# Linear attention: transposes in place of four-column fp32 matmuls for key sums and normaliser, and stages that end without GpSimd's drain

## What is computed

```python
q = hidden_states @ Wq.T + bq
k = hidden_states @ Wk.T + bk
v = hidden_states @ Wv.T + bv
...
sq = elu_plus_one(q)
sk = elu_plus_one(k)
kv = jnp.einsum('bhsd,bhse->bhde', sk, v)
qkv = jnp.einsum('bhsd,bhde->bhse', sq, kv)
k_sum = sk.sum(axis=2)
norm = jnp.einsum('bhsd,bhd->bhs', sq, k_sum)
attn = qkv / (norm[..., None] + EPS)
...
return attn @ Wo.T
```

## Time and profile before

| what | us |
|---|---|
| median of three runs | 1677.63 |
| lowest and highest run | 1674.96, 1680.66 |
| profiled execution: span from first to last instruction | 1676.2 |
| TensorE busy in it | 1602.2 |
| VectorE busy | 1156.1 |
| GpSimd busy | 637.4 |
| ScalarE busy | 414.9 |

### The profile page before, as it was taken

How to read it: one execution, slowest core, us unless ns; L and a number is a source line. 1 busy time by engine, 2 the same in 40 slices (tenths; PEclk the granted TensorE clock), 3 DMA queues, 4 the chain that set the end, 5 groups by cost and what they waited for, 6 DMA issues and landing times. The chain is left out here.

```text
span 1676.2 us, 20502 instructions
## 1 busy us (share of the span) xinstructions
PE 1602.2 (96%) x6768; PEld 1134.1 (68%) x6768; DVE 1156.1 (69%) x1641; ACT 414.9 (25%) x706; POOL 637.4 (38%) x473
## 2 busy tenths in 40 slices
PE   6999988999999989979999999999999999999997
PEld 3444456566576566558877878777776677888886
DVE  5889788788888898565537777787877556252423
ACT  2333231111111111123233333333332222121211
POOL 3686646465665576530023323232332332010101
PEclk9999999999999999999999999999999899999999
DMA  5434878755756754332200000000005433011010
GB/s 198 169 111 175 296 251 248 236 202 212 242 194 201 242 194 171 138 113 76 94 20 20 20 20 26 13 26 19 13 11 183 116 119 143 9 48 52 19 57 25
DMA packets 84388, 197.87 MB, mean 118 GB/s; under 512 B 6864, under 2 KB 28112, under 8 KB 75984
## 3 DMA queue, kind: packets, MB, share of 16 engines
q1 hardware_dynamic: 84160, 196.28, 35.0%
q10 hardware_dynamic: 144, 0.52, 0.1%
HBM read 154.83 MB, written 41.94 MB: 117 GB/s over the span
## 5 line engine op out<-in xcount | busy, mean ns | idle before, releaser
L2003 DVE SCALAR_TENSOR_TENSOR l_acc<-l_ps,l_inv,l_acc 128x512 f32<-128x512 f32 x240 | 166.1, 747 | 6.1 <-PE l_ps L768 6.1
L2530 DVE CAST g_x_part<-g_x 128x512 fp32r<-128x512 f32 x64 | 37.1, 580 | 185.0 <-ACT g_x L2582 185.0
L1879 POOL TENSOR_TENSOR relay<-l_expq,l_reluq 128x512 f32<-128x512 f32 x42 | 55.4, 1318 | 188.6 <-ACT l_expq L2163 188.6
L766 PE MATMUL r_ps<-relay_part,entry 128*128 128x512 f32 x256 | 104.8, 410 | 15.0 <-DVE r_h L1193 5.2
L2458 POOL TENSOR_TENSOR relay<-relay 128x512 f32<-128x512 f32 x16 | 21.7, 1354 | 256.0 <-DVE relay L2510 256.0
L1074 POOL TENSOR_TENSOR r_rS<-r_S,first_r 128x512 f32<-128x512 f32 x64 | 94.5, 1479 | 57.9 <-DVE r_S L1178 57.9
L1074 POOL TENSOR_TENSOR r_rS<-r_S,r_rT 128x512 f32<-128x512 f32 x64 | 95.2, 1487 | 55.8 <-DVE r_S L1178 55.1
L1979 DVE TENSOR_SCALAR l_expq<-l_ps,l_bq 128x512 f32<-128x512 f32 x64 | 48.0, 751 | 86.6 <-ACT l_reluq L2159 86.6
L766 PE MATMUL g_ps<-g_Wdn,g_x_part 128*128 128x512 f32 x256 | 103.7, 405 | 0.0
L766 PE MATMUL l_ps<-l_M_part,l_sq_part 128*128 128x512 f32 x256 | 101.8, 398 | 0.8 <-DVE l_acc L2003 0.8
L768 PE MATMUL r_ps<-relay_part,entry 128*128 128x512 f32 x256 | 101.3, 396 | 0.0
(11 more groups left out here) (332 smaller groups left out, 4081.0 us busy)
## 6 DMA issues: line engine op xcount, KB each, us to landing
entry<-scratch_wgu SPq DMA_DIRECT2D x32, 1024.0 KB, 6.1
V<-scratch_v SPq DMA_DIRECT2D x96, 256.0 KB
relay<-scratch_x SPq DMA_DIRECT2D x15, 1024.0 KB, 7.8
r_w_part<-scratch_wgu SPq DMA_DIRECT2D x12, 1024.0 KB, 7.1
scratch_wgu<-f_halves SPq DMA_DIRECT2D x24, 384.0 KB, 5.0
relay<-scratch_v SPq DMA_DIRECT2D x32, 256.0 KB
relay<-in_x SPq DMA_DIRECT2D x4, 1024.0 KB, 7.8
scratch_x<-f_xT SPq DMA_DIRECT2D x4, 1024.0 KB, 6.7
```

The costliest lines, as they stand in the source:

```text
L766: nc.tensor.matmul(out, left[1], right[0], start=start, stop=False)
L1879: nc.gpsimd.tensor_tensor(sq[i % N_SQ], expq[i % 2][:, :], reluq[i % 2][:, :], ALU.add).then_inc(sq_ready, 1)
L2003: last = nc.vector.scalar_tensor_tensor(acc[b][:, t, :], ps, scale, acc[b][:, t, :], ALU.mult, ALU.add)
L2530: nc.vector.tensor_copy(hi[:, :], x2[j % 2][:, :]).then_inc(x2_hi_ready.sem, 1)
```

## The change

The key sums and the turned rows come from four transposes each, 128 by 128, that fill a whole bank. What the stationary or moving column picked before is picked by the reader now: line 1986's operation reads every 32nd of the 512 columns (`P // B` is 32), 16 values as before. For the key sums, VectorE reads every 32nd column as four heads by four tiles and adds the four (`key_sums`, a new function), which replaces both ScalarE's copy and the constant `every` with its reduction and its semaphore. Its places in VectorE's stream are: before `values(b)` for the batch before, and for the last batch after the second `minimum` of the second part. Allocations behind `every` move by 32 bytes per partition.

```diff
-        block = ctx.enter_context(nc.Block())
+        block = ctx.enter_context(nc.Block(no_gpsimd_drain=True))
...
+            def key_sums(b):
+                dve.wait_ge(*product("ksum", b))
+                by_part = place("ksum", b)[:, 0:KVH * D:P // TT].rearrange("p (g t) -> p g t", t=TT)
+                nc.vector.tensor_reduce(ksum[b][:, :], by_part, AX.X, ALU.add).then_inc(ksum_ready, 1)
...
-                nc.vector.tensor_scalar(flat(norm[h % 2][:, :, :]), place("turn", h)[:, 0:TT * B], 1e-6, None,
+                nc.vector.tensor_scalar(flat(norm[h % 2][:, :, :]), place("turn", h)[:, 0:TT * P:P // B], 1e-6, None,
                                         ALU.add).then_inc(norm_ready, 1)
...
-            nc.vector.tensor_reduce(every[:, :], ident[:, 0:P:32], AX.X, ALU.add).then_inc(every_ready, 1)
...
+                if b > 0:
+                    key_sums(b - 1)
                 values(b)
...
+                if i == 1 - LEAD:
+                    key_sums(B - 1)
...
-            def copy_ksum(b):
-                act.wait_ge(*product("ksum", b))
-                nc.scalar.activation(ksum[b][:, :], place("ksum", b)[:, 0:KVH], ACT.Copy).then_inc(ksum_ready, 1)
...
-                if b > 0:
-                    copy_ksum(b - 1)
...
-                if i == 1 - LEAD:
-                    copy_ksum(B - 1)
...
-                    pe.wait_ge(every_ready, 1)
                     pe.wait_ge(krow_ready, n + 1)
                     for g in range(KVH):
-                        last = nc.tensor.matmul(out[:, g:g + 1], gathered[:, g * D:(g + 1) * D], every[:, :],
-                                                start=True, stop=True)
+                        last = nc.tensor.transpose(out[:, g * D:(g + 1) * D], gathered[:, g * D:(g + 1) * D], ident[:, :])
...
                     for t in range(TT):
-                        last = nc.tensor.matmul(out[:, t * B:(t + 1) * B], gathered[:, t * P:(t + 1) * P],
-                                                ident[:, 0:P:32], start=True, stop=True)
+                        last = nc.tensor.transpose(out[:, t * P:(t + 1) * P], gathered[:, t * P:(t + 1) * P], ident[:, :])
```

More of the change, by code:

```diff
@@ L1671, in linear_attention @@
         ones = sb("ones", [P, 32])
-        every = sb("every", [P, 1])
         half = sb("half", [P, TT])
@@ L1720, in linear_attention @@
         kvT_lo_ready = sem("kvT_lo_ready")
-        every_ready = sem("every_ready")
         krow_ready = sem("krow_ready")
```

## The result

The changed kernel takes **1668.76 us** (median of ten runs, 1664.67 to 1675.62), against 1677.78 us for the kernel before (ten runs beside them, 1674.37 to 1680.99). By the medians that is 9.0 us less, where 9.2 were forecast. The ratio, worked out over the runs and not from the two medians, is 0.9954 with a 95% interval of 0.9941 to 0.9966: 7.7 us less, somewhere between 5.7 and 9.9. So it is faster by 0.34 to 0.59%; that the medians meet the forecast to a few tenths of a microsecond is closer than these runs can resolve.

The account below looks back on a forecast made before the run. The prediction took TensorE in the attention to bound the kernel: -9.4 us for 20 groups, 0 for VectorE, +0.2 for barriers, -9.2 in all. That gave 1668.4 us, range 1663.5 to 1673.0.

Parts of the forecast that it names:

- What bounds the kernel: In the attention, TensorE sets the pace: a microsecond less for it is one off the end if nobody becomes late.
- The group of transposes, 0.82 to 0.35: At each turn and key sum, TensorE's group falls from 0.82 to 0.35 us, 0.47 us less.
- 20 groups, -9.4: 16 turns and 4 key sums at 0.47 us each: 9.4 us less on TensorE, bounds 7.6 to 9.6.
- VectorE, zero: In the attention, VectorE's new reductions and strided norm operation cost nothing; reductions without cover 0.8 us, at worst 1.6.
- Barriers, +0.2: At the ends of stages, the changed barriers add 0.2 us in all, bounds 0 to +0.5.
- The sum and the time: Whole kernel: -9.4 + 0 + 0.2 = -9.2 us, forecast 1668.4 us, 0.55% less.
- The clock rival: After groups of transposes the granted clock falls to 1.2 GHz; about 1718 us if after each of 20; 3%.
- VectorE does not take over: Rival judged: VectorE takes TensorE's place at each turn, giving back up to 0.47 us at 20 places; 6%.
- the transposes are one record each: Rival judged: transposes run as fp32 matmuls in two records, +1 us in all, 1678.8 us; 2%.
- the drain was not on the path: Rival judged: GpSimd's drain held back the barriers, at most 3.4 us at each of four ends; 2%.
- the low-clock stretches give something back: Rival: the half-clock stretch at the last stage's start shifts, with over 4.5 us given back; 9%.
- Marks that failed as they were worded: Signs: equal barrier distances, last stage starting about 9.2 us earlier, no stage outside the attention changing over 1 us.

Follow-up runs that it names:

- transposes_only: The changed kernel with the old ends of stages (GpSimd's drain kept): 1665.73 us, ratio 0.9941 to the kernel before.
- the empty blocks: The changed kernel with 20 empty blocks behind the last stage: 1674.82 us with GpSimd's drain, 1676.64 us without it.
- transposes_twice: The changed kernel with each of the 20 groups of four transposes issued twice into the same bank: 1676.12 us, ratio 1.0001 to the kernel before.
- barrier_only: The kernel before with only GpSimd's drain removed at all four blocks: 1677.2 us, ratio 1.0002 to the kernel before.
- matmuls_twice: The kernel before with each of the 20 groups of four narrow fp32 matmuls issued twice: 1696.35 us, ratio 1.0116 to the kernel before.

## Why the prediction was right, point by point

- **What bounds the kernel.** Right. 0.47 us less for TensorE at a head is 0.47 us less for the head (26.775 to 26.305, group start to group start). Nobody became late. The doubled groups show it from the other side.
- **The group of transposes, 0.82 to 0.35.** Right to 0.01 us: 0.35 and 0.36 in the trace. The row with the same neighbours on both sides was the one to take. The lower bound of 0.38 gained, from a long run of transposes, is what a second group costs, not the first.
- **20 groups, -9.4.** 9.4 on the ruler with the barriers kept (transposes_only). The 26.83 us of the forecast between turns was a small misreading. The first and last start of the earlier trace rows are those of the group's first and of its last record; from group start to group start it is 26.775 us. The difference hid in both kernels' rows alike.
- **VectorE, zero.** Right, though one reason was not read from the rows: that the last batch leaves VectorE more room. TensorE waits 0.9 us for VectorE's values just there, behind the third reduction. The wait is the same after the change and even with 4.1 us more ahead of it, so the reduction is free there too. The reduction takes 0.17 us, and two whole-bank reductions more before it cost nothing either. The norm operation with its stride did not become slower: 165 ns where it had 174. The idle 0.42 us ahead of the first accumulation went, and nothing else did.
- **Barriers, +0.2.** The sign and the reason were right, the term was too small: +0.3 by the two barriers round the attention (4 x 0.08), +0.4 by the empty blocks, within its bounds. 0.05 us had been put on an event with its dispatch, which no row gave; it is 0.08 to 0.1. The removal of the drain gains nothing, since SyncE is last.
- **The sum and the time.** -9.4 and +0.3 to +0.4 are -9.0 to -9.1; the medians say -9.0, the ratio -7.7 with an interval of -5.7 to -9.9. The forecast of 1668.4 is 0.4 from the median of 1668.76. That closeness is in part luck, since the ten runs of before spread over 6.6 us and those of after over 11; what carries the terms is the ruler.
- **The clock rival.** Refuted. The heads are at 1.00, with four and with eight transposes in a row. The rule of the Trainium skill (TensorE: Matmul & The Clock Gate, Part 4: PE-mode transpose), that transposes do not count as activity like matmuls, is not borne out by these runs; had it held in the way of that rival, transposes_twice would have shown it first. No run here has more than sixteen transposes in a row, so what a long stretch of them alone would do is not shown.
- **The other rivals.** VectorE does not take over; the transposes are one record each; the drain was not on the path (barrier_only 1.0002). That the low-clock stretches give something back: in the profiled execution, yes, but in the wrong place. The last stage is 2.1 us shorter there, not longer, and the front and the recurrence are 6.9 us longer.
- **Marks that failed as they were worded.** The distances at the barriers are not equal: 0.08 us longer. Two more failed by much. "The start of the last stage about 9.2 us earlier" is 1.9 us (1287.9 to 1286.0), and the front and the recurrence did not stay as long as they were. Both compare two single executions across stages that the change leaves alone, and the low-clock time differed there by some 20 us. By the forecast's own words a change of over 1 us outside the attention would have counted against it. The marks should have been set within the attention.

By mechanism the best version is transposes_only: the same groups, with barriers that are 0.1 us shorter. Its 1665.73 us (five runs) and after's 1668.76 can't be told apart by their intervals, and 0.3 to 0.4 us is all that the rows account for.

## What to carry to other kernels

To pick a few columns out of a tile on an engine that is full, a transpose of the whole tile can be cheaper than a narrow fp32 matmul, if the reader can pick the columns instead: compare the two by the time to the next product's start, in a place with the same neighbours. An engine that waits a long time in its drain costs nothing while another arrives later; look at who arrives last before taking the drain out. When a gain is under a per cent, measure between marks inside the changed stage, from the same record of each group.

## What the runs showed of the hardware

- A barrier without GpSimd's drain is dearer than one with it when GpSimd is idle: 0.44 us against 0.33. Behind stages it is 0.08 us dearer too, with SyncE last to arrive. An idle GpSimd's DRAIN takes 34 ns, where one after the recurrence took 3006 ns.
- Four fp32 matmuls with four columns run as eight records and cost 0.82 us between wide products, 0.89 us when they follow another such group. Four fp32 transposes with 128 columns cost 0.35 us, 0.44 us when they follow others.
- Reading 16 values per partition from PSUM with a stride of 32 took VectorE 165 ns, 16 neighbouring ones 174 ns.
- The granted clock can fall in a full stream of matmuls: in the profiled execution of matmuls_twice it was 0.50 for 3.4 us behind the last sixteen records of narrow matmuls, and products with 512 columns stood 0.43 us apart in place of 0.23. It was seen once, and its cause is open.
- The scatter between executions goes with stretches at half clock: in the ten runs of the changed kernel, from a span of 1662.9 us at a mean clock of 0.991 to 1673.8 us at 0.985. A stage opens at half clock, for 5.1 us in one execution and 6.3 in another.
